# Merging the last three program blocks of a graph-network and mixture-of-experts kernel into one

## The reference

```python
x = x + _L0_gnn_ref(_layernorm(x), src, dst, edge_weight, ...)   # gather 100000 edges, segment sum
x = x + _L0_ffn_ref(_layernorm(x)[None], ...)[0]                 # shared MLP and 4 small experts
x = x + _L1_gnn_ref(_layernorm(x), edge_index, edge_attr_64, ...)[...]
#   sums = segment_sum(edge_attr, src); mean = sums / max(counts, 1)
#   h = relu(concat([x, mean, u]) @ W1 + b1);  out = h @ W2 + b2
x = x + _L1_ffn_ref(_layernorm(x)[None], ...)[0]
#   top 2 of 8 gates, softmax of the two; for each expert e:
#   h = relu(x @ W1[e].T + b1[e]); y = h @ W2[e].T + b2[e]; out += combine[e] * y
```

## Time and profile before

| | us |
|---|---|
| median of three runs (3598.64 to 3603.66) | 3603.11 |
| profiled execution, its own time | 3600.04 |
| its span in the trace | 3598.3 |
| second dense part, first load issued | 2434.46 |
| its last group's rows ready for the store | 2698.64 |
| block between begins | 2750.75 |
| first transposes of the experts | 2785.29 |
| copy to the output issued | 3575.86 |

### The profile page before, as it was taken

How to read it: one execution, slowest core, us unless ns; L and a number is a source line. 1 busy time by engine, 2 the same in 40 slices (tenths; PEclk the granted TensorE clock), 3 DMA queues, 4 the chain that set the end, 5 groups by cost and what they waited for, 6 DMA issues and landing times. The chain is left out here.

```text
span 3598.3 us, 46222 instructions
## 1 busy us (share of the span) xinstructions
PE 2594.3 (72%) x10972; PEld 1965.9 (55%) x10973; DVE 1325.9 (37%) x3119; ACT 915.4 (25%) x2048; POOL 1833.2 (51%) x1911
## 2 busy tenths in 40 slices
PE   0556665666666788788777108997891999999996
PEld 0444444444544445545444008995661888888774
DVE  6322237778532212212222008973552222222232
ACT  5554333333332222222222000002420111111221
POOL 3777777777766676777777770003333222222221
PEclk9877788888897777777787558997775999999998
DMA  6333333333332112111211115536425444444313
GB/s 204 97 104 104 104 104 105 104 104 105 104 89 92 66 52 71 66 66 56 66 66 57 66 35 145 147 101 194 139 86 196 104 107 118 109 107 113 94 33 94
DMA packets 198074, 357.58 MB, mean 99 GB/s; under 512 B 47450, under 2 KB 131857, under 8 KB 195986
## 3 DMA queue, kind: packets, MB, share of 16 engines
q0 software_dynamic: 83072, 157.64, 16.9%
q1 hardware_dynamic: 112434, 182.03, 16.0%
q10 hardware_dynamic: 2528, 17.46, 1.2%
HBM read 275.03 MB, written 88.35 MB: 101 GB/s over the span
## 5 line engine op out<-in xcount | busy, mean ns | idle before, releaser
L773 POOL DMA_INDIRECT sorted_edges<-stage,sidx x784 | 753.9, 962 | 311.1 <-issue 148.7
L315 POOL DMA_INDIRECT rows<-xn_rows,idx x784 | 749.4, 956 | 300.8 <-issue 285.4
L626 PE MATMUL psum<-rows,shared 128*128 x1984 | 604.3, 466 | 364.4 <-ACT rows L366 354.6
L626 PEld LDWEIGHTS psum<-rows,shared 128*128 128x128 f32 x1984 | 447.5, 233 | 521.3 <-issue 445.8
L366 ACT ACTIVATE rows<-rows,w_c 128x256 f32<-128x256 f32 x784 | 333.9, 496 | 593.7 <-DMA rows<-xn_rows,idx 593.7
L1072 PE MATMUL psum<-hot,rows 128*65 128x128 f32 x2048 | 231.9, 275 | 185.7 <-DVE hot L1090 185.7
L1072 PEld LDWEIGHTS psum<-hot,rows 128*65 128x65 f32 x2048 | 225.1, 139 | 192.8 <-DVE hot L1090 191.8
L1619 PE MATMUL psum<-xr 128*128 128x256 f32 x1344 | 298.4, 380 | 0.9 <-DVE xr L1718 0.9
L1630 PE MATMUL psum<-fw,xr 128*128 x1344 | 297.0, 379 | 0.0
L1619 PEld LDWEIGHTS psum<-xr 128*128 128x128 f32 x1344 | 256.3, 191 | 36.3 <-DVE xr L1718 1.3
L1630 PEld LDWEIGHTS psum<-fw,xr 128*128 128x128 f32 x1344 | 252.1, 190 | 32.5
(11 more groups left out here) (306 smaller groups left out, 3302.3 us busy)
## 6 DMA issues: line engine op xcount, KB each, us to landing
xr<-in_f_W_dram SPq DMA_DIRECT2D x44, 1024.0 KB, 5.0
rows<-sorted_edges SPq DMA_DIRECT2D x260, 132.0 KB, 2.2
stage<-in_attr_dram SPq DMA_DIRECT2D x28, 924.0 KB, 4.6
fw<-in_f_W_dram SPq DMA_DIRECT2D x16, 1024.0 KB, 14.4
rows<-xn_rows,idx POOLq DMA_INDIRECT x784, 2.8
sorted_edges<-stage,sidx POOLq DMA_INDIRECT x784, 2.2
hidden_parts<-h ACTq DMA_DIRECT2D x7, 1792.0 KB, 5.8
hx<-hidden_parts SPq DMA_DIRECT2D x7, 1792.0 KB, 8.1
```

What stands on the lines that cost most here:

```text
L315: pool.indirect_dma_start(out=rows[:, c, :], out_offset=None, in_=xn_d, in_offset=bass.IndirectOffsetOnAxis(ap=idx[:, c:c + 1], axis=0)).t ...
L626: last = nc.tensor.matmul(psum[:, bank(u), 0:D], hot[:, u, c, :], rows[:, ds(slots[k] + c, 1), :].squeeze(1), start=c == 0, stop=c == RUN - 1)
L773: pool.indirect_dma_start(out=edges_d, out_offset=bass.IndirectOffsetOnAxis(ap=sidx[:, h, c:c + 1], axis=0), in_=stage[:, h, c, :], in_off ...
```

## The change

The three blocks become one. `fw1` is gone: the tile that stays on chip is `fw2`, loaded where `fw1` was, and W1 is streamed for the narrow steps too, into the same two halves of `wide_w` as for the wide ones. Rows are stored into the output itself, which has 128 rows more than before, and the experts' outputs are added there; `sum_d` and the two copies at the end are gone. So that all fits, small tiles lie inside `sums`, `hx5`, `h5`. The order of the dense part changes too: a group's normalisation statistics follow each tile's addition; the gates come one group later (`gates(g-2)`); ACT takes over `gate_columns`; `xs6` has three buffers; and on PE the transposes and the gate products of a group stand between the node products of the next one.

On SP (`sum_d` rows are the same in both directions but for the tensor's name):

```diff
 for e in range(NX):
-    sp.dma_start(fw1[:, e, :, :], a["f_W1"][e].rearrange("(c p) n -> p c n", p=P)).then_inc(s_w7, 16)
+    sp.dma_start(fw2[:, e, :, :], a["f_W2"][e].rearrange("(m p) n -> p m n", p=P)).then_inc(s_w7, 16)
...
-sp.dma_start(sum_d[(NT - G) * P:NP, :].rearrange("(t p) d -> p t d", p=P), xr[:, NT - G:NT, :]).then_inc(s_sum, 16)
+sp.dma_start(out["y"][(NT - G) * P:NP, :].rearrange("(t p) d -> p t d", p=P), xr[:, NT - G:NT, :]).then_inc(s_sum, 16)
+sp.wait_ge(s_hadd, NG * 8)
+sp.dma_start(fb2, a["f_b2"].partition_broadcast(P)).then_inc(s_w7, 16)
...
+sp.wait_ge(s_y6, NT)
+sp.wait_ge(s_tab, 3)
...
+for u in range(2):
+    weights_of(expert(u), u, s_in[u])
+sp.wait_ge(s_free, NG)
+for u in range(2):
+    load_wide(u, u)
...
+with sp.Fori(0, NBLK // 2) as it:
+    for u in range(2):
+        j = it * 2 + u
+        e = expert(j + 2 + NARROW)
+        sp.wait_ge(s_xc, j + 1 + TURNED)
+        load_narrow(j + 2, u)
+        sp.wait_ge(s_m1, j * 2 + 2 + M * NWIDE)
+        weights_of(e, u, s_wn[u])
...
-sp.dma_start(out["y"][0:HALF_N, :].rearrange("(a b) d -> a (b d)", b=ROWS), sum_d[0:HALF_N, :].rearrange("(a b) d -> a (b d)", b=ROWS)).then_inc(s_out, 16)
```

On POOL (`dispatched(g)` waits until group g's scatters have landed and then raises `s_free`):

```diff
-for g in range(NG):
+for g in range(NG - 1):
     dispatch(g)
     dispatched(g)
+dispatch(NG - 1)
...
 for e in range(NX):
     pool.indirect_dma_start(out=xd_d, out_offset=bass.IndirectOffsetOnAxis(ap=pad_i[:, e:e + 1], axis=0),
-                            in_=zero8[:, :], in_offset=None).then_inc(s_pad, 16)
-pool.wait_ge(s_pad, 16 * NX)
+                            in_=zero8, in_offset=None).then_inc(s_pad, 16)
+dispatched(NG - 1)
```

On PE (`turn` is two transposes, `logits` two products of 8 columns, `node` four of 256, `hidden` the eight products of the mean rows, `reciprocals` the two that were its head):

```diff
-    hidden(i + 1)
-    gates(i)
-    nodes(i + 1, i)
...
+for g in range(1, NG):
+    hidden(g)
+    if g + 1 < NG:
+        reciprocals(g + 1)
+    for k in range(G):
+        if k == 4 and g >= 2:
+            counts(g - 2)
+        node(g, k)
+        if k == 0 and g + 1 < NG:
+            pe.wait_ge(s_tc5, T5_BASE + (g + 1) * 2 + 2)
+        turn(g - 1, k)
+        if k:
+            logits(g - 1, k - 1)
+    logits(g - 1, G - 1)
```

On ACT and DVE, the loops over groups and DVE's end (`deviations` is the rest of the normalisation once the statistics are there; it waits for ACT's square root, `deviation`):

```diff
+for g in range(1, NG):
+    deviation(ln6, g - 1, s_v6, s_sd6)
+    gate_rows(g - 1)
+    hidden(g)
+    if g >= 2:
+        ratio(g - 2)
+    gate_columns(g - 1)
+    if g + 2 < NG:
+        act.wait_ge(s_t5, T5_BASE + (g + 1) * 2 + 2)
+        node_rows(g + 2)
...
+for g in range(1, NG):
+    deviations(g - 1)
+    add_parts(g)
+    if g + 1 < NG:
+        node_columns(g + 1)
+    if g >= 2:
+        gates(g - 2)
+    node_sums(g, range(4))
+    if g >= 2:
+        places(g - 2)
+    node_sums(g, range(4, G))
+deviations(NG - 1)
+gates(NG - 2)
+places(NG - 2)
+gates(NG - 1)
+places(NG - 1)
```

More of the change, by code:

```diff
@@ L1019, in build @@
         weights = ctx.enter_context(ExitStack())
-        fw1 = sb("fw1", [P, NX, 2, HX], f32, weights)
+        fw2 = sb("fw2", [P, NX, HX // P, D], f32, weights)
         fb1 = sb("fb1", [P, NX, HX // P], f32, weights)
@@ L1190, in _ @@
+                        for u in range(2):
+                            sp.wait_ge(s_in[u], LOADED + 16 * (NBLK // 2 + 1))
+                            sp.wait_ge(s_wn[u], 16 * (NBLK // 2 + 1))
                     @block.gpsimd
@@ new lines, in wide_transpose @@
+                        def wide_transpose(j, u, n):
+                            pe.wait_ge(s_in[u], n)
+                            if not isinstance(j, int):
+                                pe.wait_ge(s_xc, j)
+                            for c in range(2):
+                                for h in range(2):
+                                    last = nc.tensor.transpose(psum[:, 0, c * W + h * P:c * W + (h + 1) * P],
+                                                               wide_x[:, u, h, c * P:(c + 1) * P], ident[:, :])
+                            last.then_inc(s_xt, 1)
```

703 lines of the change are left out of this document (344 added, 359 removed).

## The result

The changed kernel takes 3502.67 us in the median of four runs (3499.14 to 3515.61), the kernel before 3601.94: a ratio of 0.9732, with a 95% interval of 0.9705 to 0.9759. The profiled execution took 3499.14 us, its span 3497.4.

| part | before, us | after, us | measured | predicted |
|---|---|---|---|---|
| span's start to the store of group 0 | 2472.11 | 2479.44 | +7.3 | 0 |
| group 1, store to store | 42.16 | 27.86 | -14.3 | 0 |
| groups 2 to 6 | 184.37 | 134.18 | -50.2 | -18.4 |
| last store to the experts' first transposes | 86.65 | 58.92 | -27.7 | -20.3 |
| from there to the last addition's landing | 790.57 | 790.05 | -0.5 | 0 |

A forecast was written before the change was run, and what follows sets the result against it. PE was taken to bound the dense part, at a reduced clock. Gains of 22.4 (end), 20.3 (join) and 18.4 us (groups 2 to 6) sum to 61.1; from 3600.04 that gives 3538.9, predicted as 3540, range 3515 to 3570.

The forecast's parts named there:

- the rival on the slow side: Dense part: the clock stays down throughout, 53 us a group, 3638 us; decides from 45.4 us a group; chance 0.06.
- the stores: Dense part, sign in the profile: group stores 31 to 35 us apart, with a mean PEclk of 0.85 to 0.90.
- the narrow steps: Experts: narrow steps of 8.0 us with no wait for weights, W1 landing in 5.0 us under a 12.4 us cover; cost 0.
- The dense part's content and waits, 30.2 us a group at full clock: Groups 2 to 6: 27.5 us of PE work plus 2.7 of waits make 30.2 us a group at full clock.
- the same 27.5 us of PE work: Dense part: node, hidden and gate products, reciprocals, transposes and counts keep the full-clock cost read from the old timeline.
- three waits that had not been measured: Dense part, PE waits: 1.2 us amid hidden products, 0.9 before the first node product, 0.6 before the last gate products.
- The clock, 3.0 us a group: Dense part: clock still falls in most groups but rises some 9 us sooner, 3 us lost instead of 5.8; bounds 0 and 5.8.
- the clock stays up: Rival, dense part: node products never pause for long and waits shrink, 30.2 us a group, 3525 us; chance 0.16.
- The join, 66.4 us: Group 6's rows ready to the experts' start: POOL's scatters and paddings end last, 66.4 against 86.65 us, gain 20.3 us.
- then the eight paddings, which stand ahead of the signal: Join, on POOL: eight padding transfers delay the signal for the experts' row loads, 8 x 1.28 = 10.2 us.
- The end, 22.4 us: Kernel's end: the copy with all engines idle is removed and nothing takes its place; gain 22.4 us, at least 21.5.
- Group 1, even,: Group 1: additions begin 4.7 us later behind slower fw2 load, offset by no gates round; bounds 3 us gained, 5 lost.

The follow-up runs named there:

- no_landing_wait: Changed kernel, but POOL waits tile by tile for the scatters of the group before, not for a whole group to land before going on; 3496.54 us.
- changed_again: The changed kernel itself, unchanged, run once more beside the others on the same chip; 3500.85 us, ratio 0.9729.
- block_behind: Changed kernel, with a group's transposes and gate products in one block behind the node products instead of between them; 3535.69 us, ratio 0.9824.
- block_ahead: Changed kernel, with a group's transposes and gate products in one block between the reciprocals and the node products; 3553.56 us, ratio 0.9873.
- block_hidden_128: Changed kernel with transposes and gate products in one block behind the node products and hidden products on constant operands of 128 rows; 3506.03 us, ratio 0.9726.
- the kernels with fillers: Changed kernel plus extra unread products on 128 or 64 rows amid the hidden products and behind the reciprocals, four or eight a group; 3512.07 to 3527.62 us.
- pads_behind: Changed kernel, but POOL raises the signal for the last group's scatters ahead of the eight padding transfers instead of behind them; 3505.56 us.
- before_no_copy: Kernel before, with rows stored and experts' outputs added in the output itself and the two end copies gone; 3581.20 us, ratio 0.9953.
- tail: Changed kernel with two small chained transfers added on SP at the very end; 3508.01 us.
- hidden_128: Changed kernel with the hidden products on constant operands of 128 rows in place of the 64-row mean edge rows (other numbers result); 3498.95 us, ratio 0.9710.
- rows_128: Changed kernel with the true hidden sums on 128 rows, zeros below row 64; 3501.53 us. The second also drops POOL's landing waits between groups; 3494.33 us.
- filler_64: Changed kernel with four extra unread 64-row products a group, two amid the hidden products and two behind the reciprocals; 3512.07 us.
- filler_128_long: Changed kernel with eight extra unread 128-row products a group, amid the hidden products and behind the reciprocals; 3514.68 us.

## Why the prediction was wrong

**Direction and parts** were right: every part that was forecast to gain did, and the rival on the slow side did not come near: its point was 45.4 us a group. The gain between the profiles is 39.8 us larger than predicted. Groups 2 to 6 make 31.8 of that (18.4 of content and waits, 13.4 of clock), the join 7.4, groups 0 and 1 7.0, the experts 0.5, and the end took 6.9 back. Of the signs that the prediction had named, the first transposes came after 58.92 us and not 64 to 69, and the stores stood 25.8 to 27.2 us apart and not 31 to 35; the narrow steps came as named.

**The dense part's content and waits, 30.2 us a group at full clock.** This is the step that failed most. The prediction kept "the same 27.5 us of PE work" and added waits of 2.7. At full clock groups 3 to 5 take 27.2, all five 132.6 (no_landing_wait) where 5 x 30.2 = 151 was put: 18.4 us of the miss. The 30.2 took the light work at its price in a block and three waits that had not been measured. Of the 3.0 us in a middle group, 1.7 are light work that costs 0.64 a tile between node products instead of 0.91 (25.8 us of PE work in 27.17 less 1.38 of waits), and 1.3 are waits: 0.45 and 0.93 were measured where 1.2, 0.9 and 0.6 were put. The rest is that group 2 waits only 0.22 us and group 6 has no reciprocals (1.72), and both were charged like the middle ones.

**The clock, 3.0 us a group.** The prediction had it fall "in most groups". In the profiled execution it cost 134.2 - 132.6 = 1.6 us in all instead of 15; in changed_again it cost 149.4 - 132.6 = 16.8. The size was that of one execution or another, so no single profile could confirm or refute it; the place was right (a full fall is in the hidden products, and the clock is up with the first node products), and such a fall costs 3.7 to 5.7. The rival "the clock stays up" had the profiled clock, but with 30.2 us a group it would have given 3525, and so missed as well. The prediction's reason for a shorter loss, no block of transposes and gate products behind the hidden products, is shown: block_behind and block_ahead cost 35 and 45 us against the first profile, 18 and 27 against the slowest with the changed order. That products on 128 rows in place of 64 shorten the loss is shown with the block (34 us a group against 28.4 on the mean of groups 2 to 5 in block_hidden_128), and likely without it (15 of 15 groups at full clock against 15 of 35; but the kernels with fillers kept their hidden products on 64 rows and had few falls too). What decides in which groups the clock falls with 64 rows stays open.

**The join, 66.4 us.** Every step up to the last scatter held: places ready at 14.2 (15 put), first scatter of group 5 at 15.6, last one at 2693.79 - 2641.48 = 52.3. The step that failed is "then the eight paddings, which stand ahead of the signal": the row loads were put at 63 us and came at 55.66, 3.4 us after the last scatter's row had begun at 52.3, and moving the paddings behind the signal gained nothing (pads_behind, 56.0). That is 7.4 us of the miss. The terms as written add up to 66.0, not 66.4.

**The end, 22.4 us, "at least 21.5".** The copies hid 6.95 us that every execution has behind the last addition. Measured 15.5, and 6.7 us stand there in before_no_copy and tail. The bound was wrong because the span of the kernel before could not show what ran beside its copies.

**Group 1, even,** came out a little on the gaining side of its bounds. The additions begin 3.45 us later where 4.7 were put: the second weights moved at 347 to 352 GB/s (2450 to 2466 us), not at 333. From the first load to the store of group 1 the kernel before takes 79.8 and 77.1 us in its two profiles (before_no_copy's is the second). The changed order takes 72.6 in the first profile, and 69.4 (no_landing_wait), 76.4, 76.7 and 77.0 in four others that load the weights at the same place: 4 us gained on the mean and 7.2 between the profiled executions, where a gain of 3 to a loss of 5 was allowed. The +7.3 and -14.3 of the first table are mostly one first group at half clock (12.31 against 6.28 us for its hidden products), which before_no_copy has as well and which is not the change's, and the wait in group 1 that it hides. By the Trainium skill's rule (DMA: Bandwidth & Descriptors, "Why small descriptors are slow") 1.4 us were estimated for the slower load; the 3.45 measured are larger, as the prediction expected of its rows. **The narrow steps** held to the hundredth: 7.98 us, no wait for weights.

## What to carry to other kernels

Cost work on TensorE by where it stands, not by its own duration: here small products between large ones cost 0.64 us a tile against 0.91 in a block, and a block of them ahead of products on 64 rows lost the clock with PE busy for 99% of the time. Filling the other 64 rows with zeros took no time (6.28 us for the eight either way) and may keep the clock. Before a tail is counted as a gain, ask what ran beside it; and test a load's cover again after each gain ahead of it.

## What the runs showed that I had not expected

- The eight hidden products of the first group take 6.28 us at full clock on 64 rows and on 128. But on 128 rows they ran at full clock in hidden_128 and both rows_128 kernels, and took 8.16 us in block_hidden_128; on 64 rows they took 6.28 us in four profiles (the kernel before, changed_again, filler_64, filler_128_long) and 12.31 in the other twelve.
- A first group at full clock does not pay while the second weights are loaded ahead of it: group 1 then takes 32.9 to 35.7 us instead of 25.0 to 33.7 (blocks and fillers aside), with the wait for its hidden part.
- POOL's rows of indirect transfers run behind its program: row loads that wait for a signal behind eight paddings were issued 7 us before the last padding's row. The Trainium skill (Advanced Engine Details and Errata, "Engine Queue Depths") gives GpSimd a queue of 8. That would fit the eight paddings, but no run here varied their number.
- Two executions of the same dense part differ by up to 15 us through the clock alone (134.2 and 149.4 for groups 2 to 6), so a single profile of such a part is one draw of several.
